# Layer 2's leftover rows of two blocks as four 64x64 tiles, and the pooled sums scaled by VectorE

## The reference

```python
x0 = inputs
prev = inputs
results = []
for i, f in enumerate(CIN_LAYERS):               # [128, 128, 128]
    h = prev.shape[1]                            # 39, 64, 64
    Wr = Ws[i].reshape(h, M, f)                  # M = 39
    z = jax.nn.relu(jnp.einsum('bhk,bmk,hmf->bfk', prev, x0, Wr) + bs[i][None, :, None])
    half = f // 2
    results.append(z[:, :half])
    prev = z[:, half:]
pooled = jnp.sum(jnp.concatenate(results, axis=1), axis=-1)
return pooled @ W_lin
```

## Time and profile before

| | us |
|---|---|
| median of 3 runs | 2036.53 (2036.04 to 2037.37) |
| the profiled execution's own time | 2036.55 |
| its span, first to last instruction | 2034.8 |
| PE busy | 2012.9 (99%) |
| DVE busy | 1773.4 (87%) |
| ACT busy | 539.0 (26%) |

### The profile page before, as it was taken

The page is one execution under the profiler, slowest core; times in us unless marked ns, Lnnn a source line. Parts: engine busy times, 40 slices in busy tenths (PEclk is TensorE's granted clock), DMA queues, the critical chain, the costliest instruction groups (busy, mean ns, idle before and its releaser), DMA issues.

```text
span 2034.8 us, 19288 instructions
## 1 busy us (share of the span) xinstructions
PE 2012.9 (99%) x6050; PEld 812.5 (40%) x6050; DVE 1773.4 (87%) x1118; ACT 539.0 (26%) x547; POOL 1.3 (0%) x6
## 2 busy tenths in 40 slices
PE   7999999999999999999999999999999999999998
PEld 2344333443334443344433344433444333443343
DVE  6988988889888889888898888998888988889887
ACT  1321233311333213332123331133321233311332
POOL 0000000000000000000000000000000000000000
PEclk8999999999999999999999999999999999999999
DMA  8968766678666687666786666876668866678610
GB/s 200 202 143 181 171 146 145 146 159 190 143 144 145 145 189 166 142 145 146 167 183 142 147 144 148 191 158 142 147 144 175 175 145 144 148 154 191 150 32 0
DMA packets 98552, 309.03 MB, mean 152 GB/s; under 512 B 19252, under 2 KB 19252, under 8 KB 98408
## 3 DMA queue, kind: packets, MB, share of 16 engines
q1 hardware_dynamic: 97400, 307.71, 69.2%
q10 hardware_dynamic: 1136, 1.12, 0.2%
HBM read 308.74 MB, written 0.01 MB: 152 GB/s over the span
## 4 chain that ended last, share of the span: by engine, by line
PE 96%; DVE 2%; issue 0%; ACT 0%; DVEq 0%; ACTq 0%
PE acc L369 67%; PE acc L408 26%; PE acc L363 3%; DVE prod L239 1%; DVE x_bc L212 1%; DVE prod L245 0%; DVE sum L286 0%; ACT prev L460 0%; PE acc_y L449 0%; DVE x_rot L227 0%; DVE x_seed L348 0%; ACT pool L495 0%; DVE prod L243 0%; DVEq L257 0%; ACTq L483 0%
## 5 line engine op out<-in xcount | busy, mean ns | idle before, releaser
L239 DVE TENSOR_TENSOR prod<-prev,x_bc 128x2048 f32<-128x2048 f32 x512 | 1139.0, 2287 | 7.1 <-PE acc L369 7.1
L369 PE MATMUL acc<-prod,w_sb 128*128 128x512 f32 x2432 | 1053.1, 594 | 2.4 <-DVE prod L239 2.3
L369 PEld LDWEIGHTS acc<-prod,w_sb 128*128 128x128 f32 x2432 | 459.1, 190 | 594.2 <-issue 573.5
L408 PE MATMUL acc<-prod,w_sb 128*64 128x512 f32 x2560 | 556.8, 593 | 2.0 <-ACT res L490 1.9
L245 DVE TENSOR_TENSOR prod<-prev,x_bc 128x1024 f32<-128x1024 f32 x224 | 265.5, 1221 | 231.5 <-ACT prev L460 230.5
L369 PE MATMUL acc<-x_rot,w_sb 117*128 117x512 f32 (+1 forms) x768 | 338.7, 596 | 8.7 <-DVE x_rot L227 8.7
L408 PEld LDWEIGHTS acc<-prod,w_sb 128*64 128x64 f32 x2560 | 180.8, 137 | 374.0 <-issue 333.8
L460 ACT ACTIVATE prev<-acc,bias 64x1024 f32<-64x1024 f32 x128 | 142.0, 1109 | 545.6 <-PE acc L369 544.8
L465 ACT ACTIVATE prev<-acc,bias 32x1024 f32<-32x1024 f32 x256 | 283.2, 1106 | 4.0
L227 DVE TENSOR_TENSOR x_rot<-x_rot,x_rep 117x1024 f32<-117x1024 f32 (+1 forms) x192 | 221.1, 1222 | 8.8 <-DMA x_rot<-x 8.8
L369 PEld LDWEIGHTS acc<-x_rot,w_sb 117*128 117x128 f32 (+1 forms) x768 | 146.2, 191 | 196.2 <-issue 182.7
(11 more groups left out here) (20 smaller groups left out, 49.9 us busy)
## 6 DMA issues: line engine op xcount, KB each, us to landing
x_bc<-x SPq DMA_DIRECT2D x310, 256.0 KB, 10.7
x_bc<-x SPq DMA_DIRECT2D x155, 512.0 KB, 18.7
x_rot<-x SPq DMA_DIRECT2D x192, 312.0 KB
x_rot<-x SPq DMA_DIRECT2D x192, 156.0 KB
x_bc<-x SPq DMA_DIRECT2D x124, 128.0 KB, 6.6
x_rep<-x SPq DMA_DIRECT2D x64, 192.0 KB
x_rep_s<-x SPq DMA_DIRECT2D x64, 128.0 KB, 22.0
x_rot_s<-x SPq DMA_DIRECT2D x64, 128.0 KB, 22.1
```

Of the source, the lines that this page charges most:

```text
L239: mul = nc.vector.tensor_tensor(prod[:, s:s + w, :], twice, x_bc[:, u, t:t + w, :], ALU.mult)
L369: mm = nc.tensor.matmul(acc[:, h, :], w, rhs[:, BANK * h:BANK * h + BANK], start=start, stop=stop)
L408: mm = nc.tensor.matmul(acc2[HALF * h:HALF * h + HALF, :], w2_sb[:, ORDER[pos], :], prod[:, pos % RING, BANK * h:BANK * h + BANK], start=( ...
```

## The change

1. The leftover chunk leaves `layer2`, which now runs positions 1 to 19. `product` writes the leftover products of layer 2 to a tile of its own, `left2`: those of an even block to partitions 0 to 63, those of an odd one to 64 to 127.
2. A new `layer2_left` multiplies them after the second block of a pair: two blocks by two column halves, four tiles of 64 rows by 64 columns. In the last two blocks each has its own call, with two tiles.
3. `acc2` is two banks, one for each block of a pair. `evacuate2` and `channel_sum2` of a block come two blocks later in the program.
4. The sums are scaled by DVE, right behind the channel sum, into one table `pool`: first layers 0 and 1 (tensor_scalar), later layer 2 is added to it (scalar_tensor_tensor). `weigh` on ACT is gone, and PE's last step has one table.
5. The memset of POOL and its wait are gone, as the rows it cleared are now used.
6. Position 1 of layer 2 now frees two slots of the ring, since position 0 has none.

```diff
-        acc2 = ps("acc2", [P, BANK])
+        acc2 = ps("acc2", [P, U, BANK])
@@ product
-                if w == 2:
+                if layer == 2 and t == T1:
+                    k = slice(HALF * u, HALF * u + HALF)
+                    mul = nc.vector.tensor_tensor(left2[k, :], old[k, :], new[k, :], ALU.mult)
+                elif w == 2:
@@ products2
-                    dve.wait_ge(chunk_used, first + pos + w)
+                    if pos > 0:
+                        dve.wait_ge(chunk_used, first + pos + w)
@@ channel_sum01
+                dve.wait_ge(pooled01, i + 1)
                 channel_sum(sum01, res01[a]).then_inc(sum01_ready, 1)
+                dve.wait_ge(sum01_ready, i + 3)
+                nc.vector.tensor_scalar(pool[:, bass.ds(i * BB, BB)], sum01[:], wl_col[:, 0:1], None,
+                                        ALU.mult).then_inc(pooled01, 1)
@@ channel_sum2
-                dve.wait_ge(res2_ready, i + 1)
+                dve.wait_ge(res2_ready, i + 3)
+                dve.wait_ge(pooled2, i + 1)
                 channel_sum(sum2, res2).then_inc(sum2_ready, 1)
+                dve.wait_ge(sum2_ready, i + 2)
+                dve.wait_ge(pooled01, i + 2)
+                column = pool[:, bass.ds(i * BB, BB)]
+                nc.vector.scalar_tensor_tensor(column, sum2[:], wl_col[:, 1:2], column, ALU.mult,
+                                               ALU.add).then_inc(pooled2, 1)
@@ vector, loop
                     products1(i, u, j + u, i * (2 * CH))
-                    channel_sum2(i)
+                    channel_sum2(i - 2)
@@ layer2
-                        mm = nc.tensor.matmul(acc2[HALF * h:HALF * h + HALF, :], w2_sb[:, ORDER[pos], :],
+                        mm = nc.tensor.matmul(acc2[HALF * h:HALF * h + HALF, u, :], w2_sb[:, ORDER[pos], :],
                                               prod[:, pos % RING, BANK * h:BANK * h + BANK],
-                                              start=(pos == 0), stop=(pos == CH - 1))
-                    mm.then_inc(chunk_used, 1)
+                                              start=(pos == 1), stop=False)
+                    mm.then_inc(chunk_used, 2 if pos == 1 else 1)
+            def layer2_left(blocks=range(U)):
+                for u in blocks:
+                    k = slice(HALF * u, HALF * u + HALF)
+                    for h in range(NH):
+                        mm = nc.tensor.matmul(acc2[HALF * h:HALF * h + HALF, u, :], w2_sb[k, CH - 1, :],
+                                              left2[k, BANK * h:BANK * h + BANK], start=False, stop=True)
+                mm.then_inc(acc2_full, 1)
@@ tensor, last blocks
-            layer2(LAST - 1, n + 2 * NR, range(TAIL, CH))
-            layer2(LAST, n + 3 * NR)
+            layer2(LAST - 1, 0, n + 2 * NR, range(TAIL, CH))
+            layer2_left([0])
+            layer2(LAST, 1, n + 3 * NR)
+            layer2_left([1])
@@ scalar, loop
-                    weigh2(i)
+                    evacuate2(i - 2, u, j)
                     evacuate1(i, u, i * (2 * CH) + CH)
                     evacuate0(i + 1, 1 - u)
-                    weigh01(i - 1)
-                    evacuate2(i, i * (2 * CH) + 2 * CH)
```

More of the change, by code:

```diff
@@ L83, in cin_kernel @@
         sum2 = sb("sum2", [P, BB])
-        pool01 = sb("pool01", [P, BATCH])
-        pool2 = sb("pool2", [P, BB + BATCH])
+        pool = sb("pool", [P, BATCH])
+        left2 = sb("left2", [P, NB])
         y_sb = x_seed[:, 0:BANK]
@@ L115, in cin_kernel @@
         acc0_full = sem("acc0_full")
+        acc2_full = sem("acc2_full")
         prev_ready = [sem(f"prev{l}_ready") for l in (1, 2)]
@@ L121, in cin_kernel @@
         sum2_ready = sem("sum2_ready")
-        pooled = sem("pooled")
+        pooled01 = sem("pooled01")
+        pooled2 = sem("pooled2")
         y_ready = sem("y_ready")
@@ L236, in product @@
                 old, new = prev[layer - 1][a], x_bc[:, u, t, :]
-                if w == 2:
+                if layer == 2 and t == T1:
+                    k = slice(HALF * u, HALF * u + HALF)
+                    mul = nc.vector.tensor_tensor(left2[k, :], old[k, :], new[k, :], ALU.mult)
+                elif w == 2:
                     twice = old[:].rearrange("p (o n) -> p o n", o=1).to_broadcast([P, w, NB])
                     mul = nc.vector.tensor_tensor(prod[:, s:s + w, :], twice, x_bc[:, u, t:t + w, :], ALU.mult)
-                elif layer == 1 and t == T1:
+                elif t == T1:
                     for h in range(NH):
@@ L301, in _ @@
             dve.sem_inc(sum01_ready, 2)
+            dve.sem_inc(sum2_ready, 1)
+            dve.sem_inc(pooled01, 1)
+            dve.sem_inc(pooled2, 1)
             dve.wait_ge(w0_loaded, 32)
@@ L317, in _ @@
             products1(1, 1, 1, 2 * CH)
-            channel_sum2(1)
             products0(2)
+            dve.wait_ge(small_loaded, 16 * SMALL)
             channel_sum01(0, 0)
@@ L334, in _ @@
             products1(LAST - 1, 0, STEPS - 1, n)
-            channel_sum2(LAST - 1)
+            channel_sum2(LAST - 3)
             products0(LAST)
@@ L339, in _ @@
             products1(LAST, 1, STEPS, n + CH + TAIL, TAIL)
+            channel_sum2(LAST - 2)
             products2(LAST - 1, 0, n + 2 * CH, range(TAIL_RUNS, NR))
@@ L342, in _ @@
             products2(LAST, 1, n + 3 * CH)
+            channel_sum2(LAST - 1)
+            channel_sum01(LAST, 1)
             channel_sum2(LAST)
-            channel_sum01(LAST, 1)
-            channel_sum2(NBLK)
             dve.wait_ge(y_ready, 1)
@@ L401, in layer1, with layer2 @@
                         full(acc1, w1_sb[:, c, :], prod[:, s, :], False, pos == CH - 1).then_inc(chunk_used, 1)
-            def layer2(i, runs, part=range(CH)):
-                pe.wait_ge(res2_ready, i + 1)
+            def layer2(i, u, runs, part=range(1, CH)):
+                if part[0] == 1:
+                    pe.wait_ge(res2_ready, i + 1)
                 for pos in part:
@@ L424, in _ @@
             layer0(1)
-            pe.wait_ge(w2_ready, 1)
-            layer2(0, NR)
+            pe.wait_ge(w2_loaded, 16)
+            layer2(0, 0, NR)
             layer1(1, 2 * NR)
             layer0(2)
-            layer2(1, 3 * NR)
+            layer2(1, 1, 3 * NR)
+            layer2_left()
             with pe.Fori(1, STEPS - 1) as j:
@@ L434, in _ @@
                     layer0(i + 1)
-                    layer2(i, i * (2 * NR) + NR)
+                    layer2(i, u, i * (2 * NR) + NR)
+                layer2_left()
             n = (LAST - 1) * (2 * NR)
@@ L439, in _ @@
             layer0(LAST)
-            layer2(LAST - 1, n + NR, range(TAIL))
+            layer2(LAST - 1, 0, n + NR, range(1, TAIL))
             layer1(LAST, n + NR + TAIL_RUNS, TAIL, ahead=False)
-            layer2(LAST - 1, n + 2 * NR, range(TAIL, CH))
-            layer2(LAST, n + 3 * NR)
+            layer2(LAST - 1, 0, n + 2 * NR, range(TAIL, CH))
+            layer2_left([0])
+            layer2(LAST, 1, n + 3 * NR)
+            layer2_left([1])
             pe.wait_ge(ones_ready, 1)
[L446 to L451, removed]
+            pe.wait_ge(pooled2, 1 + NBLK)
+            for q in range(P // QUAD):
+                mm = nc.tensor.matmul(acc_y[QUAD * q:QUAD * q + QUAD, :], ones[:],
+                                      pool[:, BANK * q:BANK * q + BANK], start=True, stop=True)
             mm.then_inc(y_ready, 1)
@@ L485, in evacuate1, with evacuate2 @@
                 keep01(acc1, 1, a)
-            def evacuate2(i, used):
-                act.wait_ge(chunk_used, used + RING)
+            def evacuate2(i, u, full):
+                act.wait_ge(acc2_full, full)
                 act.wait_ge(sum2_ready, i + 1)
[L490 to L504, removed]
+                nc.scalar.activation(res2[:], acc2[:, u, :], ACT.Relu, bias=bias[:, 2:3]).then_inc(res2_ready, 1)
             act.dma_start(w0_sb[:], w0).then_inc(w0_loaded, 16)
```

23 lines of the change are left out of this document (5 added, 18 removed).

## The result

| | before | after |
|---|---|---|
| median, us | 2036.15 (2035.89 to 2037.37, 5 runs) | 2026.19 (2025.62 to 2028.17, 5 runs) |
| the profiled execution's own time | 2036.55 | 2026.19 |
| its span | 2034.8 | 2024.4 |

The ratio is 0.9952 with a 95% interval of 0.9938 to 0.9967: 10 us less, 0.5%. The forecast had been 2026.0.

What follows compares the result with a forecast made beforehand. PE, busy throughout the middle of the run, was taken as the bound. From 2036.55 us, 15 pairs at 0.71 take off 10.6 and the last two blocks add 0.05: 2026.0 us, range 2023.7 to 2030.6.

Steps and rivals of the forecast that it cites:

- Four tiles in two rounds: In `layer2_left`, all four tiles start together: two rounds, 0.858 us, 1.01 with entry; each pair saves 0.71, 15 pairs 10.6.
- The row of 32-wide column tiles and that of the row tiles: Profile evidence for four tiles together: final sum's eight records in 1.07 us, L363's four in 1.13, each two rounds.
- Entry at 0.15: Change of tile shape into the 64x64 group, once per pair: 0.10 + 0.05 us, bounds zero and 0.30.
- Rivals 1 and 2: In `layer2_left`: tiles run two at a time, 2038.9 us, 7%; or one after another, 2065.5 us, 5%.
- the row of eight records in 1.09 us: Sign in the later profile: eight `layer2_left` records should last about 1.07 us; 1.9 or over 3.5 would refute.
- Rival 3: DVE becomes the bound in even blocks: 2030.5 us, or 2036.6 if the whole saving goes; 8%.
- The lead: DVE's products ready before PE's next layer 1 in even blocks: 1.01 us before, 0.15 left; PE needs 0.14.
- fits by about 0.01: At the next layer 1 after even blocks, DVE's remaining 0.15 us just covers PE's 0.14; no stall counted.
- the odd block has the old lead: Odd blocks keep DVE's earlier margin, since their layer 2 with the group ends 0.15 us later than before.
- The small instructions: DVE's two 128x64 scalings per block: 0.22 us each, bounds 0.09 and 0.69, hidden in DVE's idle 7.50 us.
- The last two blocks: End of the run, where PE waits for DVE: -0.86 + 1.01 - 0.1, together +0.05 us.
- -0.1: Final chain of evacuation, sum, scaling, final matmuls: DVE's scaling takes 0.30 us where ACT's took 0.44.

Runs made afterwards that it cites:

- the separate groups: The changed kernel with each block's leftover group of two 64x64 tiles run by itself behind its own block, nothing shared: 2042.14 us, ratio 1.0024 to the kernel before.
- the memset runs: The changed kernel with one more DVE memset behind the product for `left2`, in even blocks only (2030.59 us) or in odd blocks only (2034.72 us).
- the swapped halves: The changed kernel with the row halves of `left2` exchanged, even blocks on partitions 64 to 127, odd on 0 to 63: 2026.94 us.

## Why the prediction was right

- **Four tiles in two rounds**: held. 1.02 us for the group against 1.01 forecast, 0.70 for a pair against 0.71, 10.47 for the loop against 10.6. The row of 32-wide column tiles and that of the row tiles added up, and the separate groups show that the sharing is the whole gain.
- **Entry at 0.15**: held, and borne out by the group issued twice. The Trainium skill ("TensorEngine Tiling (Array Packing)", Key Properties) says that a change of mode drains TensorE. Read as a full drain, the last matmul's remainder, that would make the start late by an estimated 0.16. It is late by 0.09 to 0.11 in all seven kinds of change that the runs show.
- **Rivals 1 and 2** fell with the row of eight records in 1.09 us. Rival 3 did not happen, but it was close: the memset runs show that DVE, later by about 0.5 us in each even block or 0.6 in each odd one, costs 4 or 8 us.
- **The lead** was mis-sized in three places, and the errors did no harm. It is 0.24, not 0.15, since the product for `left2` has one wait where its forerunner had two. What PE needs is at most 0.12 (the swapped halves) and was 0.06 where PE did wait, not the 0.14 read in the first block, so the forecast "fits by about 0.01" was too narrow. And "the odd block has the old lead" was wrong: the last run of its own layer 2 comes 0.86 us closer as in the even block, and has only 0.21 left. Nothing in the prediction had looked there; that this sufficed was luck.
- **The small instructions**: 0.25 and 0.28 us, against 0.22. The second one also waits for its sum: in the loop DVE's next instruction comes 1.40 us behind the sum (929.65 to 931.05), where it came 0.94 us behind it before. All of it is hidden there, as the run with the scaling alone shows.
- **The last two blocks**: +0.05 forecast, +0.25 measured. The step that failed is "-0.1" for the final chain: from the evacuation's end (2018.83) to the matmuls (2020.34) are 1.51 us, as before (2029.18 to 2030.69). From the sum's end DVE's scaling takes 0.04 of wait, 0.28, and 0.15 to the first matmul, together 0.47, where 0.30 was forecast and ACT's took 0.44. The other 0.12 is the upper-half product, 1.26 us from start to start (1992.73 to 1993.99) where the step was 1.14, in a chain that DVE bounds; with its halves swapped that step was 1.14 again.

## What to carry to other kernels

Where the array is full of passes, price a matmul in rounds: a tile saves nothing by being small, only by running beside others, so look for work of two iterations that can share the rounds, and charge each change of shape (here 0.15 to 0.2 us). Before taking time from the engine that bounds the kernel, find each place where another one hands over to it, inside the shortened stage as well as behind it, and how much lead is left there; the average share of busy time hides it. Where a change is worth less than the scatter of the medians, compare a stretch of the traces that leaves out the start and the end.

## What the runs showed of the hardware that I had not expected

An instruction of VectorE on partitions 64 to 127 alone delays the next by 0.12 us compared with one on 0 to 63 (1.26 against 1.14 us from start to start); why was not tested. A VectorE instruction with a second, met wait starts 0.09 us later.

The last eight matmuls took 1.06 us in the changed kernel (its row is in the view of the end, above) and 1.94 in the run with groups apart, after the same 2.25 us of idle PE:

```profile
2035.43 1.94 PE L477 MATMUL acc_y<-pool,ones 128*32 128x512 f32 x8 [2.25 <-DVE pool L311]
```

By the windows view the granted clock was 1.00 (2.4 GHz) there in the first and 0.50 (1.2 GHz) in the second:

```profile
2020.30:2021.40 1.10, 1.06 (x8) 0.19 (x8) 0.00 (x0) 0.00 (x0) 0.00 (x0) 1.00 0.00 0
```

```profile
2035.40:2037.40 2.00, 1.94 (x8) 0.23 (x8) 0.00 (x0) 0.00 (x0) 0.00 (x0) 0.50 0.00 0
```

So the same idle time can cost 0.9 us in one execution and nothing in another. Before the change the first table's matmuls stood in that gap and its idle time was 1.32 us; whether that kept the clock up in every execution was not tried.
